# Four-layer cross-attention kernel: layer 2's queries, keys and first causal scores arranged by batch element, each with four PSUM banks of its own, and two row additions moved from GpSimd to VectorE

## The reference, cut to what matters

```python
# end of layer 1
x = x + relu(x @ W_ff1 + b_ff1) @ W_ff2 + b_ff2
x = layer_norm(x, g3, be3)
# beginning of layer 2
h = _ln(x, ln1_g, ln1_b)
q = (h @ sa_wq + sa_bq).reshape(Bx, Lx, H, HD) * scale
k = (h @ sa_wk + sa_bk).reshape(Bx, Lx, H, HD)
v = (h @ sa_wv + sa_bv).reshape(Bx, Lx, H, HD)
q = _apply_rope(q, cos, sin)
k = _apply_rope(k, cos, sin)
a = _attn(q, k, v, causal=True)      # softmax over q.k with the causal mask
x = x + (a @ sa_wo + sa_bo)
```

## Time and profile before

| | |
|---|---|
| median of 3 runs | 520.34 us (519.62 to 522.51) |
| profiled execution, its own time | 520.02 us |
| its span, first to last instruction | 518.2 us |
| TensorE busy | 414.1 us (80%) |
| VectorE busy | 354.9 us (68%) |
| ScalarE busy | 254.6 us (49%) |
| GpSimd busy | 241.1 us (47%) |
| mean granted TensorE clock | 0.864 |

### The profile page before, as it was taken

The page is one execution under the profiler, slowest core; times in us unless marked ns, Lnnn a source line. Parts: engine busy times, 40 slices in busy tenths (PEclk is TensorE's granted clock), DMA queues, the critical chain, the costliest instruction groups (busy, mean ns, idle before and its releaser), DMA issues.

```text
span 518.2 us, 8441 instructions
## 1 busy us (share of the span) xinstructions
PE 414.1 (80%) x2920; PEld 206.7 (40%) x2932; DVE 354.9 (68%) x802; ACT 254.6 (49%) x513; POOL 241.1 (47%) x378
## 2 busy tenths in 40 slices
PE   5999878898888999998998753666655668977797
PEld 3647544544335334333345530222232223433536
DVE  1756764559999012266873489999989898689552
ACT  2224434232002667634354338899977784457441
POOL 5052234565000443525010326999978897236420
PEclk9899999999999999999999995555565655689999
DMA  9500000000000000000000004798876669113301
GB/s 254 180 1 3 3 2 0 1 0 1 2 1 0 1 1 2 1 1 1 0 2 1 1 1 58 147 151 152 145 123 122 116 133 159 28 25 76 77 0 42
DMA packets 88976, 26.11 MB, mean 50 GB/s; under 512 B 81061, under 2 KB 88167, under 8 KB 88935
## 3 DMA queue, kind: packets, MB, share of 16 engines
q1 hardware_dynamic: 88935, 25.58, 25.5%
HBM read 5.61 MB, written 0.52 MB: 12 GB/s over the span
## 4 chain that ended last, share of the span: by engine, by line
PE 40%; DVE 29%; POOL 20%; issue 6%; DMA 2%; ACT 2%; POOLq 0%; DVEq 0%; ACTq 0%
POOL k_stack L574 12%; DVE k_stack L2117 9%; PE ps L849 5%; PE ps L864 4%; POOL stats L565 3%; PE ps L751 3%; DVE stats L2197 3%; PE ps L644 3%; DVE xh L1688 3%; PE ps L761 2%; DVE st L1679 2%; PE ps L641 2%; POOL rstd L484 2%; PE ps L825 2%; PE ps L927 1%
## 5 line engine op out<-in xcount | busy, mean ns | idle before, releaser
L2197 DVE TENSOR_REDUCE stats<-ps 128x2 f32<-128x1024 f32 x64 | 77.7, 1214 | 2.4 <-PE ps L1339 2.1
L1644 ACT ACTIVATE e_buf<-ps,stats,sders 128x512 f32<-128x512 f32 x88 | 67.7, 774 | 18.4 <-POOL stats L565 18.4
L1359 PE MATMUL ps<-k_stack,q_stack 128*32 128x128 bf16 x512 | 37.7, 302 | 36.9 <-DVE k_stack L2210 36.9
L574 POOL TENSOR_SCALAR k_stack<-e_buf,stats 128x512 int16<-128x512 f32 x88 | 62.7, 723 | 2.1 <-DVE stats L2204 1.5
L1490 ACT ACTIVATE e_buf<-ps 128x1024 f32<-128x1024 f32 (+3 forms) x44 | 28.2, 710 | 58.3 <-PE ps L849 58.3
L431 POOL TENSOR_SCALAR_AFFINE_SELECT e_buf<-e_buf 128x256 f32<-128x256 f32 x44 | 17.7, 411 | 66.0 <-ACT e_buf L1490 65.4
L1359 PEld LDWEIGHTS ps<-k_stack,q_stack 128*32 128x32 bf16 x512 | 21.5, 127 | 67.1 <-DVE k_stack L2210 64.5
L2117 DVE TENSOR_REDUCE k_stack<-ps 128x4 f32<-128x1024 f32 (+3 forms) x32 | 44.8, 1484 | 2.5 <-PE ps L808 2.5
L1339 PE MATMUL ps<-q_stack 32*128 32x512 bf16 x128 | 36.8, 575 | 12.2 <-ACT e_buf L1644 8.7
L482 POOL TENSOR_SCALAR rstd<-mv 128x4 f32<-128x4 f32 x18 | 4.4, 242 | 85.4 <-DVE mv L1682 85.4
L849 PE MATMUL ps<-k_stack,q_stack 32*128 32x512 f32 (+3 forms) x256 | 34.7, 478 | 0.6 <-ACT e_buf L1490 0.4
(11 more groups left out here) (281 smaller groups left out, 897.4 us busy)
## 6 DMA issues: line engine op xcount, KB each, us to landing
wsq<-in_squares SPq DMA_DIRECT2D x3, 384.0 KB, 5.2
k_stack<-k_stack SPq DMA_TRANSPOSE x64, 3.1
spread<-in_spread SPq DMA_DIRECT2D x1, 896.0 KB, 6.7
x<-in_x SPq DMA_DIRECT2D x1, 512.0 KB, 4.4
l_w<-in_L_xattn_W_ff SPq DMA_DIRECT2D x2, 256.0 KB, 7.1
l_w<-in_L_xattn_fc_w SPq DMA_DIRECT2D x2, 256.0 KB, 7.7
l_w<-in_L_xattn_ff_w SPq DMA_DIRECT2D x1, 512.0 KB, 8.7
out<-x SPq DMA_DIRECT2D x2, 256.0 KB, 2.3
```

What stands on the lines that cost most here:

```text
L574: pool.tensor_scalar(t_rows[n % TURNING][:, j, :], e_ring[n % len(e_ring)][:, j, :], stats[:, 2, c:c + 1], 0.0, ALU.mult, ALU.add).then_in ...
L1359: mm = pe.matmul(ps[BAND * band:BAND * (band + 1), 7, qb * P:(qb + 1) * P], v_band[:, kb, b, V * band + v, :], t_keys[n % len(t_keys)][:, ...
L1644: act.activation(e_ring[n % len(e_ring)][:, j, :], ps[:, 2 * (n % 3) + j, :], ACT.Exp, bias=stats[:, 1, c:c + 1], scale=sders[:, 8:9], acc ...
L2197: dve.tensor_reduce(stats[:, 0, c:c + 2], ps[:, 2 * (n % 3):2 * (n % 3) + 2, :], AX, ALU.max, negate=True).then_inc(S("ints.nm"), 1)
```

## The change

The banks of layer 2's beginning go by half: half 0 uses banks 4 to 7 (state, queries, keys, values; swapped ones in 4 and 5), half 1 banks 0 to 3. The first fill of the maxima (group 0, query blocks 1 and 0) goes to banks 4 to 7 and stands on TensorE between the second half's query and key projections and its values. `masked` on GpSimd is cut so that the one variant that this fill reads comes first. VectorE takes that fill's two maxima before the second half's rotation. The rotation is cut into `by_sines` and `rotated`, with half 0's sine products ahead of half 1's normalisation. The bias additions at the end of layer 1 are on VectorE. Of half 0's two cosine products on GpSimd the queries' waits for the bias addition of half 1, and the keys' for half 1's normalisation. The fillers stand in bank 3; the 14 ahead of the first fill are gone.

```diff
 FILL_AT = {0: 2 * P, 1: 0, 2: 0, 3: 0}
+FILL_BANK = [4] + [4 * (n % 2) for n in range(1, 3 * B * V)]
+L2_BANK = (4, 0)
...
-            def masked(b):
+            def masked(b, variants):
                 pool.wait_ge(S("L2.sa.rope"), 2 * b + 2)
-                for v in range(V):
+                for v in variants:
...
                     rstds_of("L1.ln3", h)
                     if h and stop >= 2:
                         pool.wait_ge(S("rope.loaded"), 32)
+                        pool.wait_ge(S("L1.ln3.x"), count("L1.ln3", "x") + 2)
                         by_cosines(0, qT, 0)
-                    post_norm("L1.ln3", 5, h)
-                    if h and stop >= 2:
-                        by_cosines(1, kT, 0)
                     if stop >= 2:
                         rstds_of("L2.ln1", h)
                 if stop >= 2:
+                    pool.wait_ge(S("L2.ln1.xh"), count("L2.ln1", "xh") + 2)
+                    by_cosines(1, kT, 0)
+                    masked(0, range(1))
                     for side, src in enumerate((qT, kT)):
-                        pool.wait_ge(S("L2.sa.rope"), side + 1)
                         by_cosines(side, src, 1)
-                    masked(0)
-                    masked(1)
+                    masked(0, range(1, V))
+                    masked(1, range(V))
...
+            def second_fill(n):
+                g, f = divmod(n, len(FILLS))
+                b, v = divmod(g, V)
+                bank = FILL_BANK[n]
+                pe.wait_ge(S("L2.sa.keys"), g + 1)
+                if n == 0:
+                    pe.wait_ge(S("L2.sa.vraw"), 1)
+                if n == 1:
+                    pe.wait_ge(S("heads.max"), 2)
+                if n == 2:
+                    pe.wait_ge(S("L2.sa.vraw"), B)
+                    pe.wait_ge(S("L2.sa.rope"), 2 * B)
...
-                for k in range(B):
-                    if k:
-                        keep_warm(5, 20, spare)
-                    turn_half(xh, "L2.ln1.xh", k)
-                    keep_warm(5, 3, spare)
-                    qkv("L2.sa", W["L2_xattn_sa_wq"], W["L2_xattn_sa_wk"], W["L2_xattn_sa_wv"], k)
-                    for side, src in enumerate((qT, kT)):
-                        pe.wait_ge(S("L2.sa.qk"), 2 * k + side + 1)
-                        pe.matmul(ps[:, 2 * side + k, :], swap[:, :], half(src, k), start=True, stop=True
-                                  ).then_inc(S("L2.sa.swapped"), 1)
-                keep_warm(5, 14, spare)
-                pe.wait_ge(S("L2.sa.vraw"), B)
-                pe.wait_ge(S("L2.sa.rope"), 2 * B)
-                causal_maxima()
+                pe.wait_ge(S("L1.ff.x"), count("L1.ff", "x") + 1)
+                turn_half(xh, "L2.ln1.xh", 0, bank=L2_BANK[0])
+                keep_warm(3, 3, spare)
+                second_queries_and_keys(0)
+                pe.wait_ge(S("L1.ff.x"), count("L1.ff", "x") + 2)
+                second_values(0)
+                second_swaps(0)
+                keep_warm(3, 20, spare)
+                turn_half(xh, "L2.ln1.xh", 1, bank=L2_BANK[1])
+                keep_warm(3, 3, spare)
+                second_queries_and_keys(1)
+                second_fill(0)
+                second_values(1)
+                second_swaps(1)
+                for n in range(1, len(FILL_BANK)):
+                    second_fill(n)
...
                     normal("L1.ln3", k, to=4)
+                    dve.wait_ge(S("L1.ln3.scaled"), count("L1.ln3", "scaled") + k + 1)
+                    dve.tensor_tensor(half_rows(x, k), half_rows(x, k),
+                                      spread[:, 5, :].unsqueeze(1).broadcast_to([P, QB, D]), ALU.add
+                                      ).then_inc(S("L1.ln3.x"), 1)
                     if stop >= 2:
                         moments("L2.ln1", k, "L1.ln3.x", 1)
+                        if k:
+                            by_sines(0, 0)
+                            by_sines(0, 1)
                         normal("L2.ln1", k)
...
+                rotated(0, 0)
+                rotated(0, 1)
+                fill_maxima(0)
+                for side in range(2):
+                    by_sines(1, side)
+                    rotated(1, side)
+                for n in range(1, len(FILL_BANK)):
+                    fill_maxima(n)
```

More of the change, by code:

```diff
@@ new lines, in second_fill @@
+            def second_fill(n):
[10 more added lines that the diff above has]
+                    pe.wait_ge(S("L2.sa.rope"), 2 * B)
+                if f == 0 and g >= 1:
+                    pe.wait_ge(S("heads.max"), QB * g - 1)
+                if f == 1 and g >= 1:
+                    pe.wait_ge(S("heads.max"), QB * g)
+                if f == 2 and g >= 1:
+                    pe.wait_ge(S("heads.max"), QB * g + 2)
+                for qb in FILLS[f]:
+                    c, w = FILL_AT[qb], (qb + 1) * P
+                    for j in range(BANDS):
+                        r = slice(BAND * j, BAND * (j + 1))
+                        pe.matmul(ps[:, bank + j, c:c + w], qT[r, b * N + qb * P:b * N + (qb + 1) * P],
+                                  km[r, v, b * N:b * N + w], start=True, stop=False)
+                    for j in range(BANDS):
+                        mm = pe.matmul(ps[:, bank + j, c + w - P:c + w], ident16[:, :], hide_q[:, :],
+                                       start=False, stop=True)
+                mm.then_inc(S("L2.sa.fill"), 1)
@@ new lines, in second_swaps, with second_values @@
+            def second_swaps(k):
+                for side, src in enumerate((qT, kT)):
+                    pe.wait_ge(S("L2.sa.qk"), 2 * k + side + 1)
+                    pe.matmul(ps[:, L2_BANK[k] + side, :], swap[:, :], half(src, k), start=True, stop=True
+                              ).then_inc(S("L2.sa.swapped"), 1)
+            def second_values(k):
+                for t in range(QB):
+                    o = ps[:, L2_BANK[k] + 3, t * P:(t + 1) * P]
+                    mm = pe.matmul(o, tile(xT, k * QB + t), W["L2_xattn_sa_wv"], start=True, stop=True)
+                mm.then_inc(S("L2.sa.v.mm"), 1)
@@ L1785, in single_head, with by_sines, rotated @@
                 normal("L1.ln2", 1, to=2)
+            def by_sines(k, side):
+                dve.wait_ge(S("L2.sa.swapped"), 2 * k + side + 1)
+                then(dve.tensor_tensor(half(tb, side), ps[:, L2_BANK[k] + side, :], sin_t[:, :], ALU.mult))
+            def rotated(k, side):
+                dve.wait_ge(S("L2.sa.cos"), 2 * k + side + 1)
+                dve.tensor_tensor(half((qT, kT)[side], k), half(ta, side), half(tb, side), ALU.add
+                                  ).then_inc(S("L2.sa.rope"), 1)
             def rotate(dst, raw, swapped, scale, sem, turn):
@@ L2097, in _ @@
                         normal("L2.ln1", k)
             if stop >= 2:
-                for k in range(B):
-                    for side, src in enumerate((qT, kT)):
-                        a, b = half(ta, side), half(tb, side)
-                        dve.wait_ge(S("L2.sa.swapped"), 2 * k + side + 1)
-                        then(dve.tensor_tensor(b, ps[:, 2 * side + k, :], sin_t[:, :], ALU.mult))
-                        dve.wait_ge(S("L2.sa.cos"), 2 * k + side + 1)
-                        dve.tensor_tensor(half(src, k), a, b, ALU.add).then_inc(S("L2.sa.rope"), 1)
```

53 lines of the change are left out of this document (17 added, 36 removed).

## The result

The changed kernel takes 518.89 us (median of 20 runs, 517.09 to 521.21), the kernel before 521.04 (20 runs, 519.52 to 523.13): ratio 0.9961, 95% interval 0.9947 to 0.9975. By the medians that is 2.15 us less (2.0 by the ratio), where 4.1 were forecast (516.2, with a range up to 518.0). The time is outside the range, on the side of too small a gain, and within 0.5% of the kernel before. The profiled execution took 518.07 us (span 516.14), the one of before 520.02 (span 518.17). Of the 2.7 us between 516.2 and 518.89, 0.7 is no loss of the change: the forecast started from the median of three executions of the kernel before, 520.34, and 20 of them gave 521.04. The ratios and their intervals leave out executions more than 1.5% above the fastest of the same kernel; the medians leave out none.

A forecast was written before the change was run, and what follows sets the result against it. VectorE's maxima were taken to bound the changed stretch: 2.52 us of wait and 1.74 of maxima gone, 0.14 given back, 4.1 in all. That gave 515.9, or 516.2 as a median, range 514.5 to 518.0.

The forecast's parts named there:

- What bounds the stretch: Maxima, 117.79 to 162.62 us: VectorE bounds them, busy 44.71 of 47.20 us, and TensorE keeps ahead of it.
- Bias additions and the late cosine: End of layer 1: additions on VectorE save 0.62 us per half, the waiting cosine 0.95; half 1's `xh` 2.19 earlier.
- Fillers holding the transposes: The 20 fillers behind half 0's swaps end at 105.27, 0.6 after `xh`, so only 1.60 of 2.19 us arrive.
- The first fill hides behind the key copy: Masked keys ready at 108.1, 108.6 at worst, for projections ending at 108.62: just hidden, 0.5 us to nothing spare.
- Half 1's rotation: Before the remaining maxima: ends at 115.4 us if held by GpSimd's masks, 115.05 unheld, 116.4 at the other end.
- The rest of the maxima: After the rotation: no 2.52 us wait, then 30 maxima of 43.09 us, ending at 158.5 instead of 162.62.
- The step that failed: Everything behind the maxima: same program, no transfer in the changed stretch, so all of it moves 4.1 us earlier.
- Rival 2: Layer 3, clock rise at 448 to 449 us stays put: costs up to 2 us, giving 518.2; chance 0.11.
- Rival 3: Fills of the maxima: clock falls to half while TensorE waits from 114.4 to 115.4, giving 524.4 us; chance 0.03.

The follow-up runs named there:

- The part alone: Kernel before with only the two bias additions on VectorE and GpSimd's half 0 cosine products held back: 518.70 us, ratio 0.9949.
- the version with 17: Changed kernel with nine fillers in layer 2's feed-forward waits and 17 instead of 20 fillers between the halves: 518.38 us, ratio to the kernel before 0.9945.
- the late fill: Changed kernel with nine fillers in layer 2's feed-forward waits, first fill behind the swaps, its maxima behind the rotation: 518.55 us, ratio to the kernel before 0.9962.
- the changed kernel's executions with four fillers: Changed kernel with four filler matmuls ahead of step 3 of the self-attention: 517.66 us, ratio to the kernel before 0.9936.
- the kernel before, shifted: Kernel before with eight or twelve filler matmuls inside the self-attention: 522.90 us (ratio 1.0026) and 524.73 us (1.0061).

## Why the prediction was wrong

Point by point, by its own steps:

- **What bounds the stretch** was right. VectorE's maxima end 4.10 us earlier, and C starts earlier by that.
- **Bias additions and the late cosine** were right. Half 1's `xh` was ready at 103.50 + 1.12 = 104.62 (forecast 104.65). The part alone gave 1.84 instead of 1.60.
- **Fillers holding the transposes** was right: 105.06 for 105.27, and with 17 of them B falls by 0.35. It is less than the 0.6 that I wrote since the transposes with 20 fillers already started at 105.06, not 105.27, and half 1's `xh` was ready at 104.62. The mask was not the limit: in the version with 17 it ended at 107.69 + 0.69 = 108.38, and the first fill started at 108.63, right behind the projections.
- **The first fill hides behind the key copy**: right, with a spare of 108.44 - 107.86 = 0.58 for the 0.5 foreseen (the mask ended at 107.17 + 0.69). GpSimd's cosine took 1.65 beside VectorE's sum, instead of 1.27.
- **Half 1's rotation** ends at 114.76 for 115.4, which was 0.6 too careful. The sines started at 112.10 instead of 112.31, and I took a sum held by a mask (0.36), and none was:

```profile
110.94 2.03 POOL L507 TENSOR_SCALAR q_stack<-qk,band_mask 128x512 f32<-128x512 f32 x3
```

GpSimd's three masks ended at 110.94 + 2.03 = 112.97, only 0.15 behind the start of the sum at 112.82, which took 0.69. Where the same sums met masks for longer, in the late fill, they took 1.07 and 1.13.
- **The rest of the maxima**: 43.76 us from 114.76 to 158.52 for 43.09. That ate the 0.6. A group takes 5.67 us (TensorE's fills at 122.33 and 128.01) for 5.59 before. The rows show where the 0.08 is: VectorE meets the end of the third fill.

```profile
120.67 1.14 PE L813 MATMUL ps<-q_stack,qk 32*128 32x512 f32 x8 [0.47 <-DVE k_stack L2152]
121.74 0.40 PE L816 MATMUL ps<-hide_q,ident 128*128 128x128 bf16 x4
122.17 2.29 DVE L2152 TENSOR_REDUCE k_stack<-ps 128x4 f32<-128x2048 f32 x1
```
```profile
125.26 1.14 PE L805 MATMUL ps<-q_stack,qk 32*128 32x512 f32 x8 [0.47 <-DVE k_stack L2117]
```

That fill starts 0.23 us behind the maximum ahead of it (120.44) here and 0.14 (125.12) in the kernel before, the last row; it ends at 122.14, and the maximum on it starts at 122.17, 1.73 instead of 1.66 behind the other. So at the third fill of each group TensorE does not keep ahead of VectorE, as the prediction had it do. Why the fill starts 0.09 later was not tried.
- **The step that failed** is "what follows is the same program: I move it by 4.1 as a whole". It is the same program, but TensorE's clock is not part of it. The two waits of 0.85 and 0.87 around four transposes in layer 2's feed-forward block, which cost no clock in the profile of before, cost it in both profiles of the changed kernel: 1.68 us. With D's 0.39, whose cause was not tried, that is all that is missing (4.03 + 0.07 - 1.68 - 0.39 = 2.03, the difference of the spans).
- **Rival 2** was the right kind, that the clock gives the gain back later, and held a chance of 0.11. I looked for it in layer 3, where the clock is at half in the rows, and not in the waits of 0.9 us ahead of 300 us, where it stood at full speed and so had the most to lose. The three executions known then, 519.62 to 522.51, were a sign that something of this kind is decided anew in each. The rise that the rival named did stay where it was, at 448.8 in the kernel before and 448.7 in the changed one, though D starts 2.42 us earlier; that D's 0.39 comes from it is not shown.
- **Rival 3** did not happen in this kernel, but in a version of it, at the place that it named: a wait of 1.22 us for the rotation, then fills at half clock. Its bound of "about one" for a wait that is safe was no bound: 0.85 and 0.87 with 0.66 of work between them are not safe, and 0.99 at 105.9 us was. The wait itself was 0.88 in the changed kernel (114.99), at full clock.

Shown: the gain up to the maxima, the fall of the clock and its price, and that fillers in these waits take it away, all in profiles. That the medians lack their 2 us for the same reason rests on executions with fillers, most of them on other chips. Not shown by a test of its own: that it is a matter of position. For it speak the six distances to the clock's first fall, and the changed kernel's executions with four fillers; the kernel before, shifted, never showed the fall. What in an execution decides where the clock turns stays open.

## What to carry to other kernels

A gain at one place moves all that follows against a clock whose turns need not move with the program: here one rise stayed at 448.7 to 448.8 us while the work ahead of it moved by 2.4. Where TensorE runs at full clock and has waits of about a microsecond close together, a few filler matmuls in them can be worth as much as the change; look for such pairs behind the change, not only in it. Where executions of one kernel differ by 3 us, cut the profiles at the same instructions and compare the pieces: a gain of 4.03 was plain in B with one profile each, while medians of 12 could not order versions half a microsecond apart. An edit meant as a pure delay must not open a wait.

## What was not expected of the hardware

The clock of TensorE fell for 3.4 us after 2 us with 0.66 of work in them (changed kernel, 284.8), after a wait of 1.22 (late fill, 114.8) and at the end of one of 2.39 (160.3), while across the same waits of 0.85 and 0.87 it stayed at 286 to 289 in the kernel before. Its first fall stood at 22.1, 22.0 and 22.0 us in the profiles of the kernel before, of the changed kernel and of its repeat, and at 34.2 in the profile with eight fillers behind the maxima, whose program up to there is the changed kernel's: layer 1's feed-forward sum then started at 86.73 instead of 84.74. So executions of the same instructions differ by 2 us before a kernel's own edit is reached. The Trainium skill ("TensorE: Matmul & The Clock Gate", What's actually happening) has the monitor's window free of the kernel's start; that fits falls which come at one time in one execution and at another in the next.

VectorE and GpSimd again held each other. A cosine product took 1.65 instead of 1.27 beside a sum that began first:

```profile
104.53 0.68 DVE L1820 TENSOR_TENSOR qk<-ta,tb 128x512 f32<-128x512 f32 x1
104.69 1.65 POOL L502 TENSOR_TENSOR ta<-qk,cos_t 128x512 f32<-128x512 f32 x1 [1.30 <-DVE xh L1715]
```

By the Trainium skill ("SBUF — State Buffer", Who interferes with whom) whichever issues first goes on and the other waits for its end. The traces agree but for 0.15 us: the later one grew by 0.37 where the two overlapped for 0.52 (here), by 0.36 for 0.51 (the sum at 114.22 in the kernel before), by 0.38 for 0.53 (the late fill's first sum), and by nothing for 0.15 (the sum at 112.82).
